# A transformer layer with two-of-eight routed experts: the shared expert moved as a whole behind the routed ones

## The reference

```python
x = x + attn(layernorm(x))        # 16 heads of 64; scores * strict lower-triangle mask, then softmax; @ Wr + br
flat = layernorm(x)
probs = softmax(flat @ router_w + router_b)             # 8 experts
weights = top-2 of probs, 0 elsewhere
shared = gelu(flat @ sw1 + sb1) @ sw2 + sb2             # 1024 -> 2048 -> 1024, for every token
expert_e = gelu(flat @ rw1[e] + rb1[e]) @ rw2[e] + rb2[e]
x = x + shared + sum_e weights[:, e] * expert_e
```

## Time and profile before

| | us |
|---|---|
| median of 3 runs (lowest, highest) | 1374.56 (1371.13, 1380.94) |
| the profiled execution | 1371.31 |
| its span on the slowest core, core 3 | 1369.7 |
| spans of cores 0 to 7 | 1334.7, 1359.7, 1352.1, 1369.7, 1340.4, 1359.8, 1350.6, 1337.8 |
| TensorE busy on core 3 | 1158.7 (85%) |
| ScalarE, VectorE, GpSimd busy | 502.5, 442.1, 131.0 |

### The profile page before, as it was taken

The page is one execution under the profiler, slowest core; times in us unless marked ns, Lnnn a source line. Parts: engine busy times, 40 slices in busy tenths (PEclk is TensorE's granted clock), DMA queues, the critical chain, the costliest instruction groups (busy, mean ns, idle before and its releaser), DMA issues.

```text
span 1369.7 us, 20655 instructions; the slowest of 8 cores (1334.7 to 1369.7 us)
## 1 busy us (share of the span) xinstructions
PE 1158.7 (85%) x7640; PEld 600.9 (44%) x7640; DVE 442.1 (32%) x593; ACT 502.5 (37%) x671; POOL 131.0 (10%) x226
## 2 busy tenths in 40 slices
PE   2988888877855988198896789999999999999997
PEld 1533333333312443043473556665656565654443
DVE  3546666677613660002201001010101010101456
ACT  2758888888821232030240221212122213112400
POOL 1012121122100004400000000000000000002320
PEclk9989999999986989599998899999999999999999
DMA  8699877798498534758599835974598974445995
GB/s 197 220 256 226 180 173 168 185 183 208 118 167 230 209 117 146 192 111 321 158 228 236 201 100 171 273 174 115 187 261 177 198 153 117 152 194 158 327 337 200
DMA packets 46483, 264.67 MB, mean 193 GB/s; under 512 B 6064, under 2 KB 6960, under 8 KB 40368
## 3 DMA queue, kind: packets, MB, share of 16 engines
q0 software_dynamic: 11120, 102.89, 39.6%
q1 hardware_dynamic: 34656, 159.26, 32.8%
q10 hardware_dynamic: 608, 1.18, 0.3%
HBM read 249.79 MB, written 91.23 MB: 249 GB/s over the span
## 4 chain that ended last, share of the span: by engine, by line
PE 57%; DMA 22%; DVE 7%; issue 5%; ACT 5%; another core or an unknown queue 3%; SPq 1%; DVEq 0%; ACTq 0%
PE PM L782 15%; PE PM L761 9%; DMA XTILE<-xe 9%; PE PM L722 6%; DMA XT<-xtok 5%; PE NUM L636 4%; PE PM L705 4%; PE SLOT L618 4%; PE PM L658 4%; PE DEN L641 3%; DMA yd<-YST 3%; ACT PT L1123 3%; PE PM L789 2%; DVE RC L883 2%
## 5 line engine op out<-in xcount | busy, mean ns | idle before, releaser
L1123 ACT ACTIVATE PT<-SLOT 128x1024 bf16<-128x1024 f32 (+1 forms) x320 | 262.4, 903 | 47.4 <-PE SLOT L618 46.5
L1187 ACT ACTIVATE HE_T<-PM,B1ALL 128x576 bf16<-128x576 f32 x128 | 94.8, 741 | 401.1 <-PE PM L761 401.1
L1050 DVE TENSOR_TENSOR YST<-PM,B2BC 128x512 f32<-128x512 f32 x64 | 44.2, 692 | 493.4 <-PE PM L782 460.2
L636 PE MATMUL NUM<-PT,VX 128*64 128x512 bf16 (+3 forms) x640 | 116.4, 362 | 33.9 <-DVE NS L874 33.8
L761 PE MATMUL PM<-XET,WB 128*128 128x288 bf16 x1024 | 127.6, 288 | 1.6 <-ACT XET L1166 1.3
L761 PE MATMUL PM<-XET,WA 128*128 128x288 bf16 x1024 | 126.1, 286 | 0.0
L782 PE MATMUL PM<-WA,HE_T 128*128 128x512 bf16 x512 | 114.2, 386 | 1.3 <-ACT HE_T L1187 1.2
L618 PE MATMUL SLOT<-QT,KT 64*128 64x512 bf16 (+3 forms) x640 | 100.7, 355 | 16.2 <-ACT PT L1123 14.5
L782 PE MATMUL PM<-WB,HE_T 128*128 128x512 bf16 x512 | 113.5, 385 | 0.1
L761 PEld LDWEIGHTS PM<-XET,WB 128*128 128x128 bf16 x1024 | 100.4, 98 | 28.9 <-issue 3.2
L761 PEld LDWEIGHTS PM<-XET,WA 128*128 128x128 bf16 x1024 | 99.9, 98 | 26.7 <-issue 1.6
(11 more groups left out here) (124 smaller groups left out, 1020.5 us busy)
## 6 DMA issues: line engine op xcount, KB each, us to landing
wbf<-WA SPq DMA_DIRECT2D x12, 2048.0 KB, 7.7
WA<-wbf SPq DMA_DIRECT2D x6, 4096.0 KB, 29.8
XT<-xtok SPq DMA_DIRECT2D x32, 512.0 KB, 4.2
WB<-w1cat POOLq DMA_DIRECT2D x4, 4096.0 KB, 29.3
WB<-w2cat POOLq DMA_DIRECT2D x4, 4096.0 KB, 29.0
yd<-YST SPq DMA_DIRECT2D x32, 512.0 KB, 3.1
WA<-w1cat POOLq DMA_DIRECT2D x6, 2048.0 KB, 20.5
WA<-w2cat POOLq DMA_DIRECT2D x6, 2048.0 KB, 18.2
```

The lines of the kernel that those rows point to most:

```text
L636: e.matmul(NUM[64 * hh:64 * hh + 64, lo:512], VX[:, kc * D + c * 128 + 64 * hh:kc * D + c * 128 + 64 * hh + 64], pt(n)[:, hh * 512 + lo:(h ...
L1123: e.activation(heads(pt(n), lo, 512), heads(slot(r), lo, 512), AF.Exp, scale=0.125).then_inc(expd, 1)
L1187: e.activation(HE_T[:, ht * CAP:(ht + 1) * CAP].rearrange("p (h q) -> p h q", h=2), heads(PM1[:, (n % 2) * 1024:(n % 2 + 1) * 1024], 0, CA ...
```

## The change

The shared expert is computed for all 2048 tokens behind the routed experts, in blocks of 512 tokens in the order 2, 3, 0, 1 (`LATE`). The transposed tokens 0 to 1023 (`XLN2T`, 2 MB), whose place the experts' tiles take, are stored to a scratch `xsp` and loaded again behind the last expert. Routing is done for tiles 0 to 7 inside the output projection's loop and for tiles 8 to 15 behind it, on half-size tiles; the scatters follow each half. Expert 0 no longer waits for the shared expert's matmuls; its inputs are loaded by SP when all 32 scatters and the store to `xsp` have landed. Only four matrices, the second ones of experts 2, 3, 5 and 6, are cast under attention and kept in `wbf`; all other loads of matrices are casts by GpSimd, and the four come from `wbf` on GpSimd's queue too. The buffers' turns are exchanged: even experts (and the shared one, x = 8) use `WA1`/`WA2`. `X1S`, its loads and stores, and the shared expert's copy in `wbf` go.

```diff
-AHEAD = [1, 3, 5]
+LATE = [2, 3, 0, 1]
+TILES = [4 * tt + i for tt in LATE for i in range(4)]
+HALF = NMT // 2
+EARLY = [2, 3, 5, 6]
+EARLY_AT = [2, 26, 50, 74]
+FIRST_AT = 98
...
         def run_sync(e):
...
-            for k in range(4 * len(AHEAD)):
-                e.wait_ge(ah_in[k % 2], 16 * (k // 2 + 1))
-                e.dma_start(out=wbf_rows(AHEAD[k // 4], k // 2 % 2)[:, (k % 2) * 8192:(k % 2 + 1) * 8192],
-                            in_=WA1[:, (k % 2) * 8192:(k % 2 + 1) * 8192]).then_inc(ah_out[k % 2], 16)
+            for k, x in enumerate(EARLY):
+                e.wait_ge(early_in, 16 * (k + 1))
+                e.dma_start(out=wbf_rows(x, 1), in_=WA1[:]).then_inc(early_out, 16)
...
+            e.wait_ge(tr_ev, HALF)
+            e.dma_start(out=xsp, in_=XLN2T[:, 0:NCH * 1024]).then_inc(xsp_out, 16)
             e.wait_ge(rt, RT_END)
-            for i in range(9):
...
+            e.dma_start(out=SB2BC[:], in_=b2cat[0:1, :].broadcast_to((128, D))).then_inc(sb2_in, 16)
+            e.wait_ge(scat, 16 * 2 * NMT)
+            e.wait_ge(xsp_out, 16)
+            load_rows(e, 0)
             for x in range(NE):
...
-                if x + 1 in AHEAD or x + 1 == NE:
...
+            e.wait_ge(y_ev, 9 * NE)
+            e.wait_ge(tr_mm, NMT + 5 * NE)
+            e.dma_start(out=XLN2T[:, 0:NCH * 1024], in_=xsp).then_inc(xsp_in, 16)
...
         def run_gpsimd(e):
...
+                if done in EARLY_AT:
+                    k = EARLY_AT.index(done)
+                    if k > 0:
+                        e.wait_ge(early_out, 16 * k)
+                    e.dma_start(out=WA1[:], in_=w2cat[EARLY[k] + 1]).then_inc(early_in, 16)
+                elif done == FIRST_AT:
+                    e.wait_ge(early_out, 16 * len(EARLY))
+                    e.dma_start(out=WA1[:], in_=w1cat[1]).then_inc(w1_in[0], 16)
+            e.wait_ge(x1_done, 4)
+            e.dma_start(out=WA2[:], in_=w2cat[1]).then_inc(w2_in[0], 16)
             e.wait_ge(zero_out, 16 * 3 * NE)
+            for g in range(2):
+                e.wait_ge(rt, RT_HALF * g + RT_IDX)
+                for k in range(2):
+                    for t in range(HALF * g, HALF * g + HALF):
+                        e.indirect_dma_start(xe, bass.IndirectOffsetOnAxis(IDX[:, k * NMT + t:k * NMT + t + 1], 0),
+                                             xn2(t), None).then_inc(scat, 16)
+            for x in range(1, NEXP):
+                if x == 1:
+                    e.wait_ge(op_mm, NMT)
+                else:
+                    e.wait_ge(e_mm1, 16 * (x - 1))
+                e.dma_start(out=w_first(x)[:], in_=w1cat[(x + 1) % NEXP]).then_inc(w1_in[x % 2], 16)
+                if x == 1:
+                    e.wait_ge(xn2_done, NMT)
+                    for j in range(4):
+                        e.wait_ge(x1_out[j], 16 * 4)
+                else:
+                    e.wait_ge(e_mm2, 9 * (x - 1))
+                w2 = wbf_rows(x, 1) if x in EARLY else w2cat[(x + 1) % NEXP]
+                e.dma_start(out=w_second(x)[:], in_=w2).then_inc(w2_in[x % 2], 16)
...
         def run_tensor(e):
...
             for i in range(NMT + 3):
+                if i == HALF + 6:
+                    positions(0)
...
                     e.wait_ge(tr_ev, t + 1)
+                    if t == HALF:
+                        e.wait_ge(rt, 1)
...
+            positions(1)
...
-            e.wait_ge(sw1_in, 16)
-            shared_first(0, WA1, H1S)
-            shared_first(1, WA1, H1S)
-            e.wait_ge(sw2_in, 16)
-            shared_second(0, WA2, H1S)
-            shared_second(1, WA2, H1S)
+            e.wait_ge(rt, RT_END)
...
-            e.wait_ge(w1_in, 16 * (len(AHEAD) + 1))
-            shared_first(2, WB1, H1D)
-            shared_first(3, WB1, H1D)
-            e.wait_ge(w2_in, 16 * (len(AHEAD) + 1))
-            shared_second(2, WB2, H1D)
-            shared_second(3, WB2, H1D)
+            e.wait_ge(w1_in[0], 16 * 5)
+            shared_first(0)
+            shared_first(1)
+            e.wait_ge(w2_in[0], 16 * 5)
+            shared_second(0)
+            e.wait_ge(xsp_in, 16)
+            shared_first(2)
+            shared_second(1)
+            shared_first(3)
+            shared_second(2)
+            shared_second(3)
...
         def run_vector(e):
...
+                if t == HALF + 3:
+                    choose(0)
+                elif t == HALF + 6:
+                    place(0)
             normalise2(NMT - 1)
+            choose(1)
+            place(1)
...
-            for t in range(8):
...
+            for i, t in enumerate(TILES):
+                e.wait_ge(d_in[i % 4], 16 * (i // 4 + 1))
+                x1 = ring(X1D, i % 4)
+                e.wait_ge(g_in[i % 4], 32 * (i // 4 + 1))
...
+                e.wait_ge(comb, 3 * i + 1)
...
+                e.tensor_add(x1, x1, SB2BC[:]).then_inc(comb, 1)
+                e.wait_ge(comb, 3 * i + 3)
+                for h in range(2):
+                    u = 2 * i + h
+                    e.wait_ge(s_mm2, u + 1)
+                    m = e.tensor_add(x1[:, h * 512:(h + 1) * 512], x1[:, h * 512:(h + 1) * 512],
+                                     PM2[:, (u % 2) * 512:(u % 2 + 1) * 512])
```

More of the change, by code:

```diff
@@ L160, in build_program @@
         s_mm1, s_gelu, s_mm2, s_add = sem("s_mm1"), sem("s_gelu"), sem("s_mm2"), sem("s_add")
[L161 to L166, removed]
+        xsp_out, xsp_in = sem("xsp_out"), sem("xsp_in")
+        w1_in = [sem(f"w1_in{i}") for i in range(2)]
+        w2_in = [sem(f"w2_in{i}") for i in range(2)]
+        early_in, early_out = sem("early_in"), sem("early_out")
         xe_in, b2_in, moe_done = sem("xe_in"), sem("b2_in"), sem("moe_done")
@@ L490, in run_gpsimd @@
                 done += 1
-                k = (done - 2) // 10
-                if (done - 2) % 10 == 0 and k < 4 * len(AHEAD):
-                    if k >= 2:
-                        e.wait_ge(ah_out[k % 2], 16 * (k // 2))
-                    w = w1cat if k // 2 % 2 == 0 else w2cat
-                    e.dma_start(out=WA1[:, (k % 2) * 8192:(k % 2 + 1) * 8192],
-                                in_=w[AHEAD[k // 4] + 1][:, (k % 2) * 8192:(k % 2 + 1) * 8192]).then_inc(ah_in[k % 2], 16)
-            for i in range(2):
-                e.wait_ge(ah_out[i], 16 * 2 * len(AHEAD))
@@ L502, in run_gpsimd @@
-            e.dma_start(out=WA1[:], in_=w1cat[0]).then_inc(sw1_in, 16)
-            e.wait_ge(av_mm, len(SCORES))
-            e.dma_start(out=WA2[:], in_=w2cat[0]).then_inc(sw2_in, 16)
-            e.wait_ge(rt, RT_IDX)
-            e.wait_ge(zero_out, 16 * 3 * NE)
-            for k in range(2):
-                for t in range(NMT):
-                    e.indirect_dma_start(xe, bass.IndirectOffsetOnAxis(IDX[:, k * NMT + t:k * NMT + t + 1], 0),
-                                         xn2(t), None).then_inc(scat, 16)
+                if done in EARLY_AT:
[6 more added lines that the diff above has]
+                    e.dma_start(out=WA1[:], in_=w1cat[1]).then_inc(w1_in[0], 16)
@@ L514, in run_gpsimd @@
             e.wait_ge(rt, RT_END)
             steps = e.value_load(QI[0:1, 0:1])
-            for x in range(NE):
-                if x in AHEAD:
-                    continue
-                if x >= 2:
-                    e.wait_ge(e_mm1, 16 * (x - 1))
-                e.dma_start(out=w_first(x)[:], in_=w1cat[x + 1]).then_inc(c1_in[x % 2], 16)
-                if x >= 2:
-                    e.wait_ge(e_mm2, 9 * (x - 1))
-                else:
-                    e.wait_ge(s_mm2, 16)
-                e.dma_start(out=w_second(x)[:], in_=w2cat[x + 1]).then_inc(c2_in[x % 2], 16)
@@ L1206, in run_scalar @@
                 e.reg_add(i, i, 1)
-            shared_gelu(2, H1D)
-            shared_gelu(3, H1D)
+            for k in range(4):
+                shared_gelu(k)
         with nc.Block() as block:
```

357 lines of the change are left out of this document (150 added, 207 removed).

## The result

The changed kernel takes 1396.0 us, the median of 1394.0, 1396.0 and 1403.9; here and in all medians below, executions in which the cores of a die ran longer at a lower granted clock are left out. Beside it the kernel before had a median of 1373.8 (1371.1 to 1380.9). The ratio is **1.0163, interval 1.0109 to 1.0217**: slower by 1.6%. The forecast was 1375 with a range of 1340 to 1404. The range holds the time, but the forecast is 21 us too fast, and 1396 is outside its own 1358 to 1392: what holds it is the room that was left for the slower rivals, above all C, and C was not the cause. That much was luck.

A forecast was written before the change was run, and what follows sets the result against it. TensorE, busy 85% of slowest core 3's span, was taken as the bound, its pauses as winnable. Terms -10 + 4.5 - 71.4 - 28 + 108.8 - 4.1 = -0.2 gave span 1369.5 and forecast 1375 us, range 1340 to 1404.

The forecast's parts named there:

- C: Slower rival in the experts: y stores held by casts of w1, 7 x 4 = 28 us, 1403 us; chance 0.12.
- What TensorE waits for, how a cast treats the other queue: TensorE's pauses can be won; beside a cast, the hardware queue gets about one row per cast row, 3.6 us each.
- rival A: Ahead of expert 0: inputs pass between cast rows in 11 us, expert 0 starts 46 us earlier, 1329 us; chance 0.11.
- Output projection: Tile 3 starts without the old pause, -27 us; later loads held by the cast of w2cat[1], +17; net -10 us.
- Routing's first half: Put between the projection's tiles: TensorE waits about 3 us for LS and loses about 1.5 more, +4.5 us.
- From the last logits to expert 0: Stretch falls from 169.2 to 97.8 us, inputs landing behind two casts of 57.1 us together: -71.4 us.
- T + 32.4: Last first-half scatters issued 32.4 us after the last logits (T), second half's routing hidden behind the first 16 issues.
- Attention, experts, shared expert, end: Attention unchanged; experts -28 us; whole shared expert behind them +108.8 us; one addition behind the last matmul, -4.1 us.
- B: Ahead of expert 0: inputs held by one cast only, 28.6 us less, 1346 us; chance 0.13.
- D: Slower rival in attention: mask work waits for early_out, 1375 + 4 x 5 = 1395 us; chance 0.02.
- The sum: Core 3's terms give -0.2 us, span 1369.5; another core may end 2 to 5 us behind it; 1375 us taken.

The follow-up runs named there:

- experiment 3: The changed kernel with expert 1's two casts as eight column blocks each (4 KB rows, not 32), nothing held: 1361.6 us in one run.
- Experiment 4: The changed kernel with both halves of the scatters waiting for the second half's routing: 1400.6 us in one run.
- hold_both: The changed kernel with both casts of expert 1 waiting for expert 0's inputs: 1387.7 us, ratio to the kernel before 1.0122.
- whole_early: The changed kernel, casts put behind inputs in turn, 4 KB rows from the projection on, attention's five casts whole: 1309.8 us, ratio to the kernel before 0.9644.
- experiment 5: Also in_turn: the changed kernel, 32 KB rows, no cast in the projection, each cast behind the inputs it would catch: 1350.7 us, ratio 0.9859.
- experiments 1 to 3: The changed kernel with expert 1's casts held (both; second only) or cut into column blocks: 1387.7, 1361.0 and 1361.6 us.
- experiments 5 to 8: The changed kernel with casts reordered, cut into blocks, or both (1350.7, 1354.5, 1323.3 and 1324.7 us); the kernel before with cut casts (1334.8 us).
- experiments 9 to 11: Changed kernel, reordered, thin casts except attention's: 1309.8 us; kernel before, thin casts: 1331.5; changed kernel, first half's scatters at 512 B a row: 1391.0.
- experiment 8: The kernel before with only its casts cut into eight column blocks: 1334.8 us, ratio 0.9685.

## Why the prediction was right or wrong

**What TensorE waits for, how a cast treats the other queue: right.** One row of the hardware queue for about one row of the cast holds whether the number of casts or the length of their rows is changed: 6, 31 and 56 us behind no, one and two casts, and 24 us behind two of thin rows. The Trainium skill, page "DMA: Bandwidth & Descriptors", section "Queues, rings and completion order", has typically 9 to 17 descriptors drained from a queue before the engine turns to the next one; by that the inputs' 36 rows would have been through in three or four turns, which was rival A. The 55.9 us above disagree, and so do the near equal packet counts (213 against 211 in the changed kernel, 567 against 579 in experiment 3); on this kernel's two queues the turn is about one row.

**Output projection: right in kind, some us short.** Tile 3's adding, and with it the tiles, came without a pause up to tile 5. Then one wait of 18.1 us (17 forecast) at the load issued while w2cat[1] was cast. The last logits ended at 505.1 us on core 3 and 503.7 on core 7, where the terms give 507.9 - 10 + 4.5 = 502.4. TensorE lost 14.0 us at the wait and, at a granted clock of 0.56 from 443 to 453 us, another 2.5 behind it. On core 3 it also waited 4.2 us ahead of the last tile's logits (1.1 on core 7), for a ScalarE that stood still for 3.7 us, "remote" as well. Against the kernel before, where -5.5 us was forecast, the last logits came 2.8 us earlier on core 3, 0.7 earlier on core 7 and 2.9 later on core 2.

**Routing's first half: right.** One wait for LS on TensorE, 3.4 us (about 3 forecast).

**From the last logits to expert 0: the term that failed**, in one piece. The step said that scatters of the first half run to T + 32.4 with "routing of the second half (7.3 us on VectorE and about 1.5 on TensorE)" hidden behind them. On core 7 exactly that happened: scatters over at T + 32.3, expert 0 at T + 95.1 (97.8 forecast); cores 4 to 6 have 96.1 to 97.9. On cores 0 to 3 VectorE began 3 to 16 us behind the last logits and GpSimd ran dry for 5.5 to 14.8 us; core 3's casts went out at T + 43.6 and expert 0 began at T + 108.6, that is 10.8 us later than forecast. The price of the two casts (57.1) and of the rest was right. The trace before had shown such pauses: on core 3's ScalarE, beside the scatters between 541 and 578 us, waits of 22.4 and 12.8 us that are put down to "remote", and one of 7.0 that is put down to TensorE. I took them for a part of that stage and gave a step that runs beside scatters no price for them. Experiment 4 shows, in one execution, that the scatters' presence causes the pause; on the chips of hold_both and of whole_early it was on the other die.

The -71.4 us also set a gap with these pauses, core 3's 169.2, against one without them. Before the change the gap was 158 to 169 us on cores 0 to 3 and 152 to 155 on cores 4 to 7. Like against like the change took off 60.6 us on core 3 and 56.6 on core 7.

**Attention, experts, shared expert, end: right on core 3.** Projection starts as before at 390 to 392. Core 3's experts took 545.5 us (543.5 forecast), the shared expert 222 (222.0), and behind the last matmul stands one addition (before there were four operations there, additions and products, and not three; the -4.1 us don't depend on it):

```profile
1381.30 0.69 DVE L1071 TENSOR_TENSOR WB<-WB,PM 128x512 f32<-128x512 f32 x1 [1.02 <-PE PM L706]
```

**Rivals.** A and B are out by 55.9 us. C hardly reached TensorE in the changed kernel: VectorE waited for y stores 14.0 us in all on core 3 (8.1 in the earlier trace rows, which leaves out expert 0) and 22.2 on core 2, and 0.8 us of core 2's reached TensorE. It is real all the same, 14 and 10 us in experiment 5. D did not happen.

**The sum.** Core 3: 13.5 us at expert 0's start (2.7 + 10.8) and 2.0 in the experts make 1385.0 of 1369.5; the span is 1385.1. From core 3 to the slowest I allowed 4 us, and core 2 is 7.3 behind it: 3.2 by a longer projection pause (17.4 us on TensorE against 14.0), -2.5 in the gap, 6.1 in the experts, where late inputs cost TensorE 8.0 us against core 3's 2.6, and 0.5 in the rest. That gives 1394.0, and the median is 2 higher.

Why is core 2 the last, which before was 17.6 us ahead of core 3? The forecast took its gains from the core that had most to gain. From the first expert to the shared one core 3 became 26.0 us shorter (571.5 to 545.5, -28 forecast), but core 2 only 9.6 (561.2 to 551.6) and cores 0 and 1 7.3 and 5.8, for they had lost less there before. What the change adds behind the experts was nearly the same for all (99.6 to 107.9 us). So the cores drew level above the old slowest one, and 2 to 5 us for the others was too little.

Where did the gain go? Behind the last logits the shared expert's first half had covered routing, scatters and casts. Put behind the experts it costs there what it costs anywhere (108.8 us), while the stretch that it left shrank only by 60.6 on core 3 (169.2 to 108.6), for it is two casts long. The experts' shorter time (-26.0 on core 3, -28 forecast) would fill that up to about zero there but for the late routing, 10.8 of the 15.4 us that core 3 lost. Over all eight cores the stretch shrank by 55 to 61 us and the experts by 6 to 37, while what comes behind them grew by 100 to 108: no core came out even.

## What to carry to other kernels

Before work is moved away from a wait, ask what the wait is made of: here it was not data volume alone but the length of the rows on the other queue, and cutting 4 MB casts into eight column blocks took 2.6 to 3.2% off the kernel before, without moving any work. A transfer that is held back to free one victim meets the next (hold_both, in_turn): shorten its rows first, then order it. Issues cost the issuing engine (0.53 us each here), so leave transfers whole where that engine's other work is awaited and nothing small shares the queues. And make the sum on more than the slowest core: the one that has most to gain is not the one that will end last.

## What the runs showed of the hardware that I had not expected

- Beside indirect scatters that GpSimd issues, VectorE and ScalarE of the cores of one die pause. In the changed kernel VectorE stood idle for 6 to 22 us on cores 0 to 3, 3 to 16 of them with the logits already there, and the trace names no releaser; on cores 4 to 7 it went on 0.2 us behind the logits. Which die it is went with the chip and not with the kernel: cores 4 to 7 in the three profiles of experiments 1 to 3, cores 0 to 3 in all four of experiments 5 to 8, cores 4 to 7 in all three of experiments 9 to 11, cores 0 to 3 in the kernel before and in the changed one, whose chip isn't on record.
- What it waits for stays open. The scatters' pace doesn't tell the dies apart: they follow each other at 1.27 us on cores 0, 2, 4 and 6 and at 1.23 on the others. Neither do packets of the instruction queues: none lies in the pause of core 2 and one in that of core 3, while cores 4 to 7 have two each from 508 to 516 us and no pause. Not having the scatters there ends it, and with 512 B rows in place of 2 KB it is 4 to 6 us beyond the logits.
- A wait that the trace puts down to a y store behind two whole matrices of its own queue went away when only the other queue's rows were made thinner (experiment 8).
